# Attention's mix and gates: one plain fp32 matmul in place of three matmuls on split operands

## The reference

```
mn  = layernorm(m) * gamma + beta
q, k, v = (mn @ Wq), (mn @ Wk), (mn @ Wv)        # 8 heads of 32
g   = sigmoid(mn @ Wg + bg)
att = einsum('slhc,tlhc->sth', q, k) * scale     # 4 x 4 per head, summed over all tokens
att = softmax(att, axis=1)
o   = einsum('sth,tlhc->slhc', att, v) * g
out = o @ Wo + bo
```

## Time and profile before

| | us |
|---|---|
| median of 3 runs | 1367.71 (1365.78 to 1368.36) |
| the profiled execution | 1368.57 |
| its span, first to last instruction | 1366.8 |
| second pass, from the first L280 to the last L295 | 279.38 to 481.85 |

### The profile page before, as it was taken

How to read it: one execution, slowest core, us unless ns; L and a number is a source line. 1 busy time by engine, 2 the same in 40 slices (tenths; PEclk the granted TensorE clock), 3 DMA queues, 4 the chain that set the end, 5 groups by cost and what they waited for, 6 DMA issues and landing times.

```text
span 1366.8 us, 19336 instructions
## 1 busy us (share of the span) xinstructions
PE 1176.2 (86%) x6707; PEld 762.5 (56%) x6707; DVE 781.3 (57%) x1514; ACT 435.6 (32%) x672; POOL 319.8 (23%) x199
## 2 busy tenths in 40 slices
PE   2799555489999968887888799999879999999997
PEld 0334344289999933333333499999744444444443
DVE  1999477643333465666675558888635544444441
ACT  1010111122222333433344323333224445444443
POOL 1000377730000242232230223333401112111100
PEclk8899798689999988998899879999959999999998
DMA  8971300000000000000000000000000001000201
GB/s 172 201 172 22 73 0 0 1 2 0 0 0 0 0 24 1 1 0 0 0 0 0 1 17 20 23 23 23 1 0 1 1 0 36 10 0 0 46 1 32
DMA packets 34232, 30.95 MB, mean 23 GB/s; under 512 B 28880, under 2 KB 30544, under 8 KB 32400
## 3 DMA queue, kind: packets, MB, share of 16 engines
q1 hardware_dynamic: 33696, 29.77, 9.7%
q10 hardware_dynamic: 432, 0.59, 0.1%
q0 software_dynamic: 64, 0.07, 0.0%
HBM read 25.57 MB, written 4.82 MB: 22 GB/s over the span
## 4 chain that ended last, share of the span: by engine, by line
PE 65%; DVE 14%; issue 9%; POOL 8%; ACT 2%; DMA 1%; DVEq 0%; SPq 0%; POOLq 0%; ACTq 0%
PE ps L552 10%; PE ps L561 9%; PE ps L280 7%; PE ps L1446 6%; PE ps L492 4%; PE ps L295 4%; PE ps L283 3%; PE ps L473 3%; POOL rot L1283 3%; PE ps L544 3%; POOL ln_rs L374 3%; PE ps L431 3%; DVE hc L904 2%; PE ps L483 2%; PE ps L640 2%
## 5 line engine op out<-in xcount | busy, mean ns | idle before, releaser
L1176 ACT ACTIVATE hc<-ps 128x768 f32<-128x768 f32 x176 | 133.3, 808 | 169.8 <-PE ps L552 169.8
L950 DVE SCALAR_TENSOR_TENSOR zc<-ztm,ps 128x384 f32<-128x384 f32 x176 | 89.6, 550 | 153.7 <-PE ps L544 153.7
L374 POOL TENSOR_TENSOR ln_rs<-ln_ve,nhalf 128x12 f32<-128x12 f32 x44 | 100.0, 2272 | 258.0 <-DVE ln_ve L394 206.9
L552 PE MATMUL ps<-zc,gw1x 64*128 64x384 f32 x704 | 139.9, 516 | 0.0
L561 PE MATMUL ps<-hc,gw 128*64 128x384 f32 x704 | 132.8, 499 | 0.0
L904 DVE TENSOR_TENSOR hc<-hact,ps 128x768 f32<-128x768 f32 x88 | 83.8, 952 | 81.0 <-PE ps L483 73.1
L399 POOL TENSOR_TENSOR lnbuf<-hid,ln_mean 128x768 f32<-128x768 f32 x22 | 32.3, 1472 | 388.7 <-DVE ln_mean L387 388.6
L785 DVE TENSOR_TENSOR zs<-sig,ps 128x384 f32<-128x384 f32 x88 | 48.7, 554 | 122.4 <-ACT sig L1085 122.4
L1141 ACT ACTIVATE hact<-ps,fb 128x768 f32<-128x768 f32 x88 | 79.2, 899 | 98.1 <-PE ps L473 98.0
L1446 PE MATMUL ps<-ring,ident 128*128 128x512 f32 x224 | 99.1, 604 | 5.5 <-DVE ring L1542 2.5
L1085 ACT ACTIVATE sig<-ps,bgc 128x384 f32<-128x384 f32 x88 | 51.1, 581 | 153.6 <-PE ps L283 153.6
(11 more groups left out here) (208 smaller groups left out, 2255.0 us busy)
## 6 DMA issues: line engine op xcount, KB each, us to landing
rows<-in_x_rows_dram SPq DMA_DIRECT2D x24, 528.0 KB, 11.6
tabc<-in_tables_dram SPq DMA_DIRECT2D x11, 384.0 KB, 3.0
out_dram<-hid SPq DMA_DIRECT2D x8, 384.0 KB, 5.0
xch<-in_x_dram SPq DMA_DIRECT2D x2, 1024.0 KB, 9.6
lnbuf<-in_x_dram SPq DMA_DIRECT2D x2, 1024.0 KB, 22.1
wdyn<-dynamic_weights SPq DMA_DIRECT2D x8, 144.0 KB, 3.3
out_dram<-hid SPq DMA_DIRECT2D x4, 256.0 KB, 3.7
gw<-in_L_ffn_W_dram SPq DMA_DIRECT2D x3, 256.0 KB, 4.3
```

The source lines that it names most:

```text
L374: p.tensor_tensor(ln_rs[:, par], ln_ve[:, par], nhalf[:, :], ALU.pow).then_inc(S(ph + "rs_ready"), 1)
L552: mm = pe.matmul(ps[:, 2 * (u % 2) + h, 0:TW], gw1x[half[h], P * e:P * e + P], zc[half[h], u % 4, :], start=True, stop=True)
L950: v.scalar_tensor_tensor(zc[:, u % 4, :], ztm[:, par, u // 8, :], 1.0, ps[:, 4 + u % 2, 0:TW], ALU.add, ALU.mult).then_inc(S("xzc_ready"), 1)
L1176: s.activation(hc[:, u % 4], ps[:, b:b + 2, 0:TW], ACT.Relu).then_inc(S("xh_act"), 1)
```

## The change

The turned tokens are copied once, as plain fp32 (`ztA`); `low`, its semaphore `zt_split` and the splits of the gate weights and of `wmix` go. Each of the three products of a round is one fp32 matmul on `wmix` or `wgp` and `ztA` in place of three float32r matmuls. PE's wait before it overwrites the turned bank is now for ACT's copy (`z1h_ready`), and PE waits once for all 11 copies before the scores.

```diff
--- before.py
+++ after.py
@@ -160,15 +160,12 @@
         attn = ExitStack()
         with attn:
             zs1 = sb("zs1", [P, 2, GW], F32, attn)
-            ztH = sb("ztH", [P, 2, NT * P], F32R, attn)
-            ztL = sb("ztL", [P, 2, NT * P], F32R, attn)
+            ztA = sb("ztA", [P, 2, NT * P], F32, attn)
 
             wk2 = sb("wk2", [P, 256], F32, attn)
             wq2 = sb("wq2", [P, 256], F32, attn)
             wv2 = sb("wv2", [P, 256], F32, attn)
             wgp = sb("wgp", [P, 2, 256], F32, attn)
-            wgH = sb("wgH", [P, 2, 256], F32R, attn)
-            wgL = sb("wgL", [P, 2, 256], F32R, attn)
             wo = sb("wo", [P, 2, D], F32, attn)
             bgc = sb("bgc", [P, 2], F32, attn)
             gramS = sb("gramS", [P, 2, 256], F32, attn)
@@ -177,8 +174,6 @@
             at = sb("at", [P, P], F32, attn)
             at2 = sb("at2", [P, P], F32, attn)
             atm = sb("atm", [P, 4 * HEADS], F32, attn)
-            wmH = sb("wmH", [P, B, 2, 256], F32R, attn)
-            wmL = sb("wmL", [P, B, 2, 256], F32R, attn)
             sig = sb("sig", [P, 2, TG * P], F32, attn)
         wmix = prodX[:, :, :].rearrange("p (s r) c -> p s r c", s=B)
 
@@ -229,7 +224,7 @@
                 z = zs1[:, par].rearrange("p (t b d) -> p t b d", b=B, t=TG)
                 pe.wait_ge(S("z1_ready"), g + 1)
                 if late(g, 2):
-                    pe.wait_ge(S("zt_split"), g - 1)
+                    pe.wait_ge(S("z1h_ready"), g - 1)
                 for pair in range(2):
                     for t in range(TG):
                         mm = pe.transpose(ps[:, 2 + 2 * par + pair, P * t:P * t + P], z[:, t, 2 * pair:2 * pair + 2, :].rearrange("p b d -> p (b d)"), ident[:, :])
@@ -246,6 +241,7 @@
             steps(pe, lambda g, par, ahead, far: back(g, par))
 
             pe.wait_ge(S("gram_out"), 1)
+            pe.wait_ge(S("z1h_ready"), NG)
             pe.wait_ge(S("attw_in"), 16 * 10)
             for m in range(2):
                 for t in range(B):
@@ -274,13 +270,9 @@
                             pe.wait_ge(S("og_ready"), 8 * g + k - 1)
                         cs = slice(P * mc, P * mc + P)
                         tok = bass.ds(g * TG * P, TG * P) if not isinstance(g, int) else slice(g * TG * P, (g + 1) * TG * P)
-                        n = 0
                         for pair in range(2):
-                            for w, z in ((wmH, ztH), (wmH, ztL), (wmL, ztH)):
-                                pe.matmul(ps[:, mc, 0:TG * P], w[:, s, pair, cs], z[:, pair, tok], start=(n == 0), stop=(n == 5))
-                                n += 1
-                        for n, (w, z) in enumerate(((wgH, ztH), (wgH, ztL), (wgL, ztH))):
-                            mm = pe.matmul(ps[:, 2 + mc, 0:TG * P], w[:, s % 2, cs], z[:, s // 2, tok], start=(n == 0), stop=(n == 2))
+                            pe.matmul(ps[:, mc, 0:TG * P], wmix[:, s, pair, cs], ztA[:, pair, tok], start=(pair == 0), stop=(pair == 1))
+                        mm = pe.matmul(ps[:, 2 + mc, 0:TG * P], wgp[:, s % 2, cs], ztA[:, s // 2, tok], start=True, stop=True)
                         mm.then_inc(S("mix_ready"), 1)
                     if late(g, 1) or s >= 1:
                         project(4 * g + s - 1, (s - 1) % 2, (s - 1) % 2)
@@ -710,15 +702,6 @@
             outputs(TG * NG - 1, TG - 1)
 
         def attn_v(v, once):
-            def low(g, par):
-
-                v.wait_ge(S("z1h_ready"), g + 1)
-                tok = bass.ds(g * TG * P, TG * P) if not isinstance(g, int) else slice(g * TG * P, (g + 1) * TG * P)
-                for pair in range(2):
-                    ins = v.tensor_tensor(ztL[:, pair, tok], ps[:, 2 + 2 * par + pair, 0:TG * P], ztH[:, pair, tok].bitcast(F32), ALU.subtract)
-                ins.then_inc(S("zt_split"), 1)
-
-
             def var(g, par):
                 ln_var_v(v, "a", g, par, (1.0 + EPS) / D, EPS * EPS)
 
@@ -731,7 +714,6 @@
                     ln_stats(v, "a", far, par)
                 if far is not None:
                     var(far, par)
-                low(g, par)
 
             ln_stats(v, "a", 0, 0)
             var(0, 0)
@@ -743,8 +725,6 @@
             v.tensor_copy(gramS[:, :, :], ps[:, 0:2, 0:256]).then_inc(S("gram_out"), 1)
             v.wait_ge(S("attw_in"), 16 * 10)
             link = once
-            link(v.tensor_scalar(wgH[:, :, :], wgp[:, :, :], 1.0, None, ALU.mult))
-            link(v.tensor_tensor(wgL[:, :, :], wgp[:, :, :], wgH[:, :, :].bitcast(F32), ALU.subtract))
             v.wait_ge(S("x_ready"), 1)
             for h in range(2):
                 link(v.tensor_tensor(prodX[:, 4 * h:4 * h + 4, :].rearrange("p (s r) c -> p r s c", r=2), ps[:, 4 + 2 * h:6 + 2 * h, :].rearrange("p r (s c) -> p r s c", s=2),
@@ -770,9 +750,7 @@
                         r = slice(64 * h, 64 * h + 64)
                         ins = v.tensor_tensor(wmix[r, s, pair, :].rearrange("p (h c) -> p h c", c=HC), wv2[r, :].rearrange("p (h c) -> p h c", c=HC),
                                               b4[r, s, 2 * pair + h, :].unsqueeze(2).to_broadcast([64, HEADS, HC]), ALU.mult)
-            link(ins)
-            link(v.tensor_scalar(wmH[:, :, :, :], wmix[:, :, :, :], 1.0, None, ALU.mult))
-            v.tensor_tensor(wmL[:, :, :, :], wmix[:, :, :, :], wmH[:, :, :, :].bitcast(F32), ALU.subtract).then_inc(S("wmix_ready"), 1)
+            ins.then_inc(S("wmix_ready"), 1)
             v.wait_ge(S("bo_added"), 1)
 
             def gate(g, between=()):
@@ -1062,7 +1040,7 @@
             def high(g, par):
                 tok = bass.ds(g * TG * P, TG * P) if not isinstance(g, int) else slice(g * TG * P, (g + 1) * TG * P)
                 s.wait_ge(S("z1_turned"), g + 1)
-                s.activation(ztH[:, :, tok], ps[:, 2 + 2 * par:4 + 2 * par, 0:TG * P], ACT.Copy).then_inc(S("z1h_ready"), 1)
+                s.activation(ztA[:, :, tok], ps[:, 2 + 2 * par:4 + 2 * par, 0:TG * P], ACT.Copy).then_inc(S("z1h_ready"), 1)
 
             def step(g, par, ahead, far):
                 if far is not None:
```

## The result

The changed kernel takes 1391.01 us (1389.91 to 1392.39, 4 runs) where the kernel before takes 1368.03 (1365.78 to 1369.64, 4 runs): ratio 1.017 with a 95% interval of 1.0151 to 1.0188, 23.0 us slower. The profiled execution took 1389.91 us, its span is 1388.2.

The account below looks back on a forecast made before the run. PE alone was taken to bound the second pass, with DVE the chain ahead of it. 1368.57 + 31.4 - 5.9 - 0.85 = 1393.2 us, or 1392.4 after the median's 0.86 below that execution; range 1386 to 1399.

Parts of the forecast that it names:

- The second pass, +31.4: Mix and gate products on PE: 12 fp32 records (3.874 us) replace 18 float32r (3.160) a round, 44 rounds, +31.4 us.
- The step on the line between 256 and 512 columns: Second pass: 384-column fp32 records cost 0.3228 us each, read between measured rows of 256 and 512 columns.
- the cheap record: Rival for the second pass: fp32 records at 0.189 us, as in L561, so the change gains, 1322 us; chance 0.03.
- a lower clock: Rival for the second pass: the fp32 stream is granted 0.88 throughout, 31 us more, 1423; chance 0.03.
- exposed weights: Rival for the second pass: each fp32 record waits for its weights, step 0.339 us, 8.4 us more, 1401; chance 0.06.
- The estimate of +42 us by passes alone: Second pass, from the skill page: each product goes from 3 to 4 passes of 0.160 us, +42 us; not adopted.
- The serial part, -5.9: Ahead of the second pass: 2.25 us gained at the subtraction behind POOL's additions, 3.61 from dropping wmix's split; -5.9 us.
- The first pass, 0: Where the turned tokens are split: POOL's power hides `low` on DVE, so dropping it costs and gains nothing.
- The end, -0.85: Before the second pass's last projection: later statistics meet less of POOL's chain, so PE idles less; -0.85 us, bounds 0 and 1.34.

Follow-up runs that it names:

- e1: The changed kernel with DVE's subtraction for the tokens' low part put back, result unused, and PE waiting for it again: 1392.3 us.
- e7: The changed kernel with POOL's four bias additions split, two left in place and two only after wmix is written: 1387.5 us.
- e6: The kernel before without the third matmul of each product (low weights by high tokens), 12 float32r records a round in place of 18: 1321.7 us.
- e2: The changed kernel with all three splits (tokens, gate weights, wmix) put back, results unused, so only the matmuls differ from the kernel before: 1398.2 us.
- e3: The changed kernel without POOL's four additions of the output bias, left out of the computation: 1393.2 us.
- e5: e4 with the gate products cut to 64 rows, two sequences in turn on the two halves of the array: 1357.6 us.
- e4: The kernel before, split matmuls kept, with the weight splits moved off the path and wmix written and split one sequence at a time: 1362.4 us.
- e8: e4 with POOL's bias additions split as in e7 and the sigmoid's table loaded before wmix is written: 1358.5 us.
- e9: e5 with both changes of e8, and the half-array gate products in one block per two rounds in place of two: 1343.2 us.

## Why the prediction was right

The forecast was 1392.4 us, 24.7 above the median then known; measured were 1391.0, 23.0 above the kernel before.

- **The second pass, +31.4.** Right, as was its reason. The step on the line between 256 and 512 columns came out at 0.3225 us against 0.3228; the passage took 30.43 us more with the shorter end included, where the two terms were 31.4 - 0.85 = 30.55. Neither the cheap record, nor a lower clock, nor exposed weights appeared. The Trainium skill, in "FP8 and Floating Point Precision", section "TensorE Precision Notes", gives true fp32 four passes through the array. The estimate of +42 us by passes alone was too high: a float32r record took 0.016 us besides its 0.160, an fp32 record 0.0025 besides 0.320. The trace decides.
- **The serial part, -5.9.** The mechanism was right at both places: L741 ended with POOL's additions, and the wait for the split of `wmix` went whole. From PE's score products to the first mix the time fell from 279.38 - 252.47 = 26.91 us to 273.01 - 251.15 = 21.86, 5.05 less. Up to the multiplications it fell by 2.22, as the sum had it (2.25). Behind them it fell by 2.83 and not by 3.61, because the multiplications met POOL's preparations and took 0.75 us more, a collision that the earlier start brought about and that I did not count.
- **The first pass, 0.** Right: the groups are as far apart as before (e1).
- **The end, -0.85.** PE's idle time fell by 1.05 us, for the reason given: the statistics (L394 before, L386 after) end with POOL's addition in both kernels, and they now begin 0.94 us after that addition began, in place of 0.23.
- **What the sum did not have.** These terms make 30.43 - 5.05 = +25.4 us in the profiled executions, where the sum had 24.65. The profiled span grew by 21.4. The other 4.0 us lie outside the terms, and most of them go with the clock that TensorE was granted. First, PE reached the score products 1.32 us sooner. 0.94 of that are the last group's twelve products for the table, which took 3.78 us at 0.78 of full speed in place of 4.72 at 0.61. e7, which lacks `low` as the changed kernel does, took 4.52 for them, and e6, which has it, 3.86; so this does not follow `low`. Second, the rest of the span, behind the second pass, was 2.66 us shorter on the same code. Counted from the start of the last projection record, it was 885.2, 885.2 and 885.3 us in the kernel before, e2 and e7, whose granted clock was 0.74 over the first 40 us from there; 882.6 and 882.5 in the changed kernel and e3, at 0.83; and 889.0 in e5, at 0.68. The five others lie between, 884.5 to 886.9 at 0.70 to 0.74, and not in strict order of that clock. Why an execution gets one clock or another stays open: no run here tried it.

## What to carry to other kernels

Price a change of number format by its steps in the stream of the engine, not by instructions: one fp32 matmul of 384 columns is two records of 0.3225 us, dearer than three float32r records of 0.1756 us, though it looks like a third of the work. Look for the gain where the split is made: dropping it gave back about 7 us and added 30 in the stream, while moving it off the serial path, with two waits of POOL and ACT out of the way, made the kernel 8 us faster than before and added nothing to the stream (e4, e8). When an instruction is set free earlier, ask what it now runs beside: e3 gave back all that it won.

## What the runs showed of the hardware beyond that

- DVE instructions with two operands in SBUF lose more beside a stream of POOL work than one wait: sixteen of 0.42 us took 15.09 us beside POOL's preparations (e3) and 6.92 without them (e7). Beside one cast of 1.04 us they took 7.67 (the changed kernel).
- Float32r records on the two halves of the array run side by side at 0.17 us a pair, but a block of them among whole-array records cost 0.38 us besides in e5 and 0.40 in e9.
